# Attention of the first layer rewritten: float32r score operands in two row tiles, a ring of three PSUM banks, no fold on TensorE

## The reference, cut to what matters

```python
q = (xn @ Wq + bq).reshape(B, S, H, dk).transpose(0, 2, 1, 3)
k = (xn @ Wk + bk).reshape(B, S, H, dk).transpose(0, 2, 1, 3)
v = (xn @ Wv + bv).reshape(B, S, H, D).transpose(0, 2, 1, 3)
scores = jnp.einsum('bhsd,bhtd->bhst', q, k) / jnp.sqrt(dk)
p = jax.nn.softmax(scores, axis=-1)
att = jnp.einsum('bhst,bhtd->bhsd', p, v)
out = att.reshape(S, B, D, H).sum(axis=-1).reshape(B, S, D)
```

## Time and profile before

| | us |
|---|---|
| median of 3 runs | 879.9 |
| lowest and highest | 877.4, 882.49 |
| span of the profiled execution | 885.5 |
| TensorE busy | 692.1 |
| VectorE busy | 523.8 |
| ScalarE busy | 306.9 |
| GpSimd busy | 292.2 |

### The profile page before, as it was taken

How to read it: one execution, slowest core, us unless ns; L and a number is a source line. 1 busy time by engine, 2 the same in 40 slices (tenths; PEclk the granted TensorE clock), 3 DMA queues, 4 the chain that set the end, 5 groups by cost and what they waited for, 6 DMA issues and landing times. The chain is left out here.

```text
span 885.5 us, 18398 instructions
## 1 busy us (share of the span) xinstructions
PE 692.1 (78%) x7232; PEld 418.3 (47%) x7232; DVE 523.8 (59%) x898; ACT 306.9 (35%) x563; POOL 292.2 (33%) x369
## 2 busy tenths in 40 slices
PE   4431899999999999969999985986962559746784
PEld 2210334333353444357677764765441548645463
DVE  3572666556666775054545533334899699655873
ACT  2310554446645655522332322553010002122431
POOL 4313041000000023233455451138994000415773
PEclk9665778668898988869999996997896555557987
DMA  3246111111111110000000001001220100000000
GB/s 101 71 139 179 50 45 48 42 36 36 49 53 42 44 47 19 1 0 1 1 1 1 1 1 25 1 14 39 48 49 27 27 4 4 2 0 1 12 13 24
DMA packets 41204, 28.72 MB, mean 32 GB/s; under 512 B 23344, under 2 KB 32560, under 8 KB 41136
## 3 DMA queue, kind: packets, MB, share of 16 engines
q1 hardware_dynamic: 39984, 26.57, 10.6%
q10 hardware_dynamic: 1152, 1.18, 0.4%
HBM read 21.35 MB, written 6.29 MB: 31 GB/s over the span
## 5 line engine op out<-in xcount | busy, mean ns | idle before, releaser
L456 DVE TENSOR_REDUCE mx<-ps 128x1 f32<-128x1024 f32 x128 | 155.7, 1224 | 83.0 <-PE ps L566 80.6
L423 ACT ACTIVATE prob<-ps 128x512 f32<-128x512 f32 x256 | 139.4, 599 | 148.1 <-PE ps L578 146.8
L578 PE MATMUL ps<-qst,kst 99*128 99x512 bf16 x256 | 96.0, 455 | 19.4 <-DMA qst<-shift_sb 19.2
L598 PE MATMUL ps<-prob,vst 128*32 128x256 f32 x1024 | 98.7, 463 | 0.4 <-ACT prob L423 0.4
L717 POOL TENSOR_TENSOR h_lo<-hf,h_hi 128x512 fp32r<-128x512 f32 x48 | 63.6, 1338 | 69.4 <-DVE h_hi L747 69.4
L565 PE MATMUL ps<-km,qm 48*128 48x512 bf16 x128 | 59.1, 463 | 16.4 <-DMA km<-k_scratch 10.0
L578 PEld LDWEIGHTS ps<-qst,kst 99*128 99x128 bf16 x256 | 24.3, 113 | 88.4 <-ACT prob L423 63.1
L608 PEld LDWEIGHTS ps<-fold_sel,q_rest 128*128 128x128 f32 x256 | 62.1, 334 | 7.4 <-issue 7.4
L608 PE MATMUL ps<-fold_sel,q_rest 128*128 128x32 f32 x256 | 64.0, 407 | 0.8 <-ACT q_rest L429 0.8
L791 PE MATMUL ps<-h_hi,w_lo 128*128 128x512 f32 x144 | 58.4, 405 | 7.7 <-issue 5.4
L747 DVE CAST h_hi<-hf 128x512 fp32r<-128x512 f32 x48 | 41.7, 896 | 38.0 <-ACT hf L690 37.4
(11 more groups left out here) (257 smaller groups left out, 1292.0 us busy)
## 6 DMA issues: line engine op xcount, KB each, us to landing
qm<-q_scratch SPq DMA_DIRECT2D x32, 64.0 KB
km<-k_scratch SPq DMA_DIRECT2D x32, 64.0 KB
w_raw<-L_ffn_h_w SPq DMA_DIRECT2D x2, 1024.0 KB, 9.4
q_scratch<-qsplit SPq DMA_DIRECT2D x4, 384.0 KB, 2.5
k_scratch<-ksplit SPq DMA_DIRECT2D x4, 384.0 KB, 2.5
qst<-q_scratch SPq DMA_DIRECT2D x16, 96.0 KB
kst<-k_scratch SPq DMA_DIRECT2D x16, 96.0 KB
X<-L_attn_x SPq DMA_DIRECT2D x4, 256.0 KB, 4.9
```

What stands on the lines that cost most here:

```text
L423: nc.scalar.activation(prob[:, u, :], expp[:, u % 2, :], ACT.Exp, scale=SCORE_SCALE).then_inc(exp_done, 1)
L456: nc.vector.tensor_reduce(mx[:, p, k:k + 1], maxp[:, k % 2, :], AX.X, ALU.max).then_inc(max_done, 1)
L578: nc.tensor.matmul(expp[:, u % 2, :], kst[0:99, p, P * t:P * t + P], qst[0:99, p, 512 * s:512 * s + 512], start=True, stop=True).then_inc( ...
L598: last = nc.tensor.matmul(pvp[32 * j:32 * j + 32, g // 2, cols], vst[:, p, u % 8, :], prob[:, u, cols], start=(g % 2 == 0 and part == 0), ...
```

## The change

The two blocks become one, and everything is written out in 144 steps.

- q and k are kept in two float32r parts (hi from ScalarE, the rest by one VectorE operation out of PSUM). Scratch holds hi, lo, hi of q and hi, hi, lo of k, so that 48 rows give hi*hi + lo*hi + hi*lo. Both matmul kinds use the same operand, which lies twice in SBUF, in rows 0 to 47 and 64 to 111, with two rows of the shift behind each (rows 48, 49 and 112, 113). Four heads' operands fit, one set of 4 DMAs each.
- The two score matmuls of a step (key tile t; queries 0 to 511 and 512 to 1023) use row tiles 0 and 64. Results go in turn to a ring of three banks, which the transposed shift uses as well.
- A value product's four column tiles are four quarters of the queries, accumulated over the eight key tiles, so no fold is needed: VectorE transposes 32 x 32 blocks from PSUM and takes the reciprocal; GpSimd multiplies and adds.
- The maximum comes negated; GpSimd splits the shift in two parts; four DMAs bring it. Scores of head h begin 13 steps behind its first row scores.
- SP issues the FFN's weights ahead of the first shift, and those of the third layer behind it. Score operands of a head are loaded three heads ahead.

```diff
-    q_scratch = nc.dram_tensor("q_scratch", (3, B, P, S), BF16, kind="Internal").ap()
+    q_scratch = nc.dram_tensor("q_scratch", (3, B, P, S), F32, kind="Internal").ap()
...
+    STACKS = 4
+    PROBS = 6
+    RING = 3
+    LAG = 5
+    PV_LAG = 2
+    MAXB, RINGB, PVB = 0, 4, 7
...
+        def score_step(h, t):
+            return 8 * (h + 1) + LAG + t
+
+        def pv_step(h, t):
+            return score_step(h, max(t, 1)) + PV_LAG
+
+        def shift_step(h):
+            return 8 * (h + 1) + 1
...
+            def load_stacks(h):
+                b, p = h // 8, h % STACKS
+                rows = slice(DK0 * (h % 8), DK0 * (h % 8) + DK0)
+                if h % 8 == 0:
+                    sp.wait_ge(splits_stored[2 * b], 4 * 16)
+                    sp.wait_ge(splits_stored[2 * b + 1], 4 * 16)
+                if h >= STACKS:
+                    sp.wait_ge(ring_psum, ring["score", h - STACKS, 7, 1] + 1)
+                for r in (0, 64):
+                    sp.dma_start(qst[r:r + 48, p, :].bitcast(F32), q_scratch[:, b, rows, :]).then_inc(stack_in[p], 16)
+                    sp.dma_start(kst[r:r + 48, p, :].bitcast(F32), k_scratch[:, b, rows, :]).then_inc(stack_in[p], 16)
+
+            def load_shift(h):
+                sp.wait_ge(ring_done, ring["shift", h] + 1)
+                for r in (48, 112):
+                    for j in range(2):
+                        sp.dma_start(qst[r + j:r + j + 1, h % STACKS, :].bitcast(F32),
+                                     shift_sb[8 * j:8 * j + 8, h % 2, :].bitcast(F32)).then_inc(shift_in, 16)
...
+            store_splits(0)
+            store_splits(1)
+            load_stacks(0)
+            store_splits(2)
+            load_stacks(1)
+            store_splits(3)
+            load_stacks(2)
...
+            for o, name in ((W1, "w1"), (W2, "w2")):
+                sp.dma_start(w_raw[:, o:o + FH], dr[f"L0_ffn_{name}_w"]).then_inc(w_in, 16)
...
+            for h in range(NH):
+                load_shift(h)
+                if h + 3 < NH:
+                    load_stacks(h + 3)
...
+            for i, unit in enumerate(ring_order):
+                act.wait_ge(ring_psum, i + 1)
+                if unit[0] == "shift":
+                    h = unit[1]
+                    if h >= 2:
+                        act.wait_ge(shift_in, 64 * (h - 1))
+                    nc.scalar.copy(shift_sb[:, h % 2, :], ps[0:16, RINGB + i % RING, 0:P]).then_inc(ring_done, 1)
+                else:
+                    _, h, t, half = unit
+                    n = 8 * h + t
+                    if n >= PROBS and half == 0:
+                        act.wait_ge(pv_done, n - PROBS + 1)
+                    nc.scalar.activation(prob[:, n % PROBS, GT * half:GT * half + GT], ps[:, RINGB + i % RING, :], ACT.Exp,
+                                         scale=SCORE_SCALE).then_inc(ring_done, 1)
...
+            def split_shift(h):
+                pool.wait_ge(max_done, 8 * (h + 1))
+                if h >= 2:
+                    pool.wait_ge(ring_psum, ring["shift", h - 2] + 1)
+                link(nc.gpsimd.tensor_copy(nsplit[:, h % 2, 0:8], nmx[:, h % 2, :]))
+                nc.gpsimd.tensor_tensor(nsplit[:, h % 2, 8:16], nmx[:, h % 2, :], nsplit[:, h % 2, 0:8].bitcast(F32),
+                                        ALU.subtract).then_inc(shift_split, 1)
+
+            def finish_head(h):
+                pool.wait_ge(folded_ready, 2 * h + 2)
+                f = folded[:, h % 2]
+                link(nc.gpsimd.tensor_tensor(att[:], f[:, :, 0:DK0], rsum[:].rearrange("p (m o) -> p m o", o=1).broadcast_to([P, 8, DK0]), ALU.mult))
+                tile = X[:, h, :]
+                nc.gpsimd.tensor_tensor(tile, tile, att[:].rearrange("p m e -> p (m e)"), ALU.add).then_inc(out_added, 1)
...
+            def left_over(g):
+                dve.wait_ge(q_hi, g + 1)
+                nc.vector.scalar_tensor_tensor(qsp[:, g % 2, 1, :], ps[:, Q_BANK, :], bq[:, 0:1], qsp[:, g % 2, 0, :].bitcast(F32),
+                                               ALU.add, ALU.subtract).then_inc(q_lo, 1)
+                dve.wait_ge(k_hi, g + 1)
+                nc.vector.scalar_tensor_tensor(ksp[:, g % 2, 1, :], ps[:, K_BANK, :], bk[:, 0:1], ksp[:, g % 2, 0, :].bitcast(F32),
+                                               ALU.add, ALU.subtract).then_inc(k_lo, 1)
...
+            def row_max(h, k):
+                s = 8 * h + k
+                dve.wait_ge(max_psum, s + 1)
+                if k == 0 and h >= 2:
+                    dve.wait_ge(shift_split, h - 1)
+                pair = ps[:, MAXB + 2 * (s % 2):MAXB + 2 * (s % 2) + 2, :].rearrange("p c t -> p (c t)")
+                nc.vector.tensor_reduce(nmx[:, h % 2, k:k + 1], pair, AX.X, ALU.max, negate=True).then_inc(max_done, 1)
+
+            def fold(h):
+                dve.wait_ge(pv_done, 8 * (h + 1))
+                if h >= 2:
+                    dve.wait_ge(out_added, h - 1)
+                f = folded[:, h % 2]
+                nc.vector.transpose(f.rearrange("p m e -> p (m e)"), ps[:, PVB, 0:256]).then_inc(folded_ready, 1)
+                dve.wait_ge(folded_ready, 2 * h + 1)
+                if h >= 1:
+                    dve.wait_ge(out_added, h)
+                nc.vector.reciprocal(rsum[:], f[:, :, DK0]).then_inc(folded_ready, 1)
+
+            for step in range(LAST + 2):
+                if step < 8 * NH:
+                    row_max(step // 8, step % 8)
+                for h in range(NH):
+                    if pv_step(h, 7) == step:
+                        fold(h)
...
+            def row_scores(h, k):
+                s, p = 8 * h + k, h % STACKS
                 if k == 0:
+                    pe.wait_ge(stack_in[p], 64 * (h // STACKS + 1))
+                if s >= 2:
+                    pe.wait_ge(max_done, s - 1)
+                bank = MAXB + 2 * (s % 2)
+                nc.tensor.matmul(ps[:, bank, :], qst[0:48, p, P * k:P * k + P], kst[0:48, p, 0:GT], start=True, stop=True)
+                nc.tensor.matmul(ps[:, bank + 1, :], qst[64:112, p, P * k:P * k + P], kst[64:112, p, GT:S],
                                  start=True, stop=True).then_inc(max_psum, 1)
...
+            def shift_to_rows(h):
+                i = ring["shift", h]
+                pe.wait_ge(shift_split, h + 1)
+                if i >= RING:
+                    pe.wait_ge(ring_done, i - RING + 1)
+                nc.tensor.transpose(ps[0:16, RINGB + i % RING, 0:P], nsplit[:, h % 2, :].bitcast(F32), ident[:]).then_inc(ring_psum, 1)
+
+            def scores(h, t):
+                p = h % STACKS
+                if h == 0 and t == 0:
+                    pe.wait_ge(ones_in, 2 * 16)
+                if t == 0:
+                    pe.wait_ge(shift_in, 64 * (h + 1))
+                for half in range(2):
+                    i, r = ring["score", h, t, half], 64 * half
+                    if i >= RING:
+                        pe.wait_ge(ring_done, i - RING + 1)
+                    nc.tensor.matmul(ps[:, RINGB + i % RING, :], kst[r:r + 50, p, P * t:P * t + P], qst[r:r + 50, p, GT * half:GT * half + GT],
+                                     start=True, stop=True).then_inc(ring_psum, 1)
...
+            def pv(h, t):
+                n = 8 * h + t
+                pe.wait_ge(ring_done, ring["score", h, t, 1] + 1)
+                if n == 0:
+                    pe.wait_ge(ones_set, 2)
+                    pe.wait_ge(v_ready, GROUPS)
+                if t == 0 and h >= 1:
+                    pe.wait_ge(folded_ready, 2 * h - 1)
                 for j in range(4):
+                    last = nc.tensor.matmul(ps[32 * j:32 * j + 32, PVB, 0:256], vp[:, h, t, :], prob[:, n % PROBS, 256 * j:256 * j + 256],
+                                            start=(t == 0), stop=(t == 7), skip_group_check=True)
+                last.then_inc(pv_done, 1)
+
+            for step in range(LAST + 1):
+                for h in range(NH):
+                    for t in range(8):
+                        if score_step(h, t) == step:
+                            scores(h, t)
+                if step == shift_step(0):
+
+                    pe.wait_ge(q_lo, GROUPS)
+                    pe.wait_ge(k_lo, GROUPS)
+                    pe.wait_ge(xnT_ready, GROUPS)
+                if step < 8 * NH:
+                    row_scores(step // 8, step % 8)
+                for h in range(NH):
+                    if shift_step(h) == step:
+                        shift_to_rows(h)
+                    for t in range(8):
+                        if pv_step(h, t) == step:
+                            pv(h, t)
```

More of the change, by code:

```diff
@@ L161, in _ @@
+        ring_order = sorted(ring, key=ring.get)
         @block.sync
@@ L244, in _ @@
             rstd(0)
-            for g in range(GROUPS):
-                if g + 1 < GROUPS:
-                    rstd(g + 1)
-                for i in range(2):
-                    pool.wait_ge(q_rounded, 3 * g + i + 1)
-                    src = qf[:] if i == 0 else q_rest[:, 0]
```

(23 more changed lines are left out.)

499 lines of the change are left out of this document (140 added, 359 removed).

## The result

The changed kernel takes 829.4 us (median of 4 runs, 817.6 to 839.1); the kernel before, timed beside it, 880.4 (877.4 to 882.5). The ratio is 0.933, 95% interval 0.925 to 0.941: faster by 51 us in the medians, where 135 were forecast, and 29 us above the top of the range. The profiled execution took 825.4 us at a span of 823.7.

The account below looks back on a forecast made before the run. TensorE was taken to bound the scores' stage. First score 57.5 + steps 170 + last steps 15 + end 3 = 245.5 instead of 380.2, so 885.5 - 134.7 = 750.8 of span, 745 us timed; 8-in-10 range 712 to 800.

Parts of the forecast that it names:

- the stacks of heads 0 to 2: Start, after the stores: SyncE issues these operand loads, 4 issues of 0.7 us each, ending near 39.5 us.
- the change of scale at the end of the sum: End of the sum: profiled span is 5.6 us above the timed median, so 750.8 becomes 745 us.
- The start: Before the scores: first score at 57.5 us instead of 90.8, gaining 33 us; bounds 52 and 66.
- The shift's row: Once a head: arrives 6.1 to 7.1 us after the maximum; TensorE waits 0.8 to 1.8, taken as 0.8.
- The clock: Scores' loop: TensorE at the low level a tenth of the time, adding 0.5 us a head.
- a step: Scores' loop, one step: 1.21 us at 2.4 GHz instead of 1.43; 2.09 at 1.2 GHz instead of 2.52.
- pairs in float32r side by side: Scores' loop: a step's two score matmuls share the array, taking away 0.21 us; weight loads cost nothing extra.
- a head: Scores' loop: 8 x 1.21 + 0.8 + 0.8 = 11.3 us at 2.4 GHz, 11.8 with the low level.
- A: Scores' loop: float32r pairs don't run side by side, 0.43 us more a step, +38: 783 us; chance 0.16.
- B: Scores' loop: less dense streaming lowers TensorE's clock; half the time low 769 us, all 827; chance 0.15.
- C: Scores' loop: VectorE alone sets the pace, 9.85 us a head, -28: 717 us; chance 0.12.
- D: Scores' loop: neither pair shares the array and the clock stays low, 2.95 us a step: 939 us; chance 0.02.

Follow-up runs that it names:

- e5: The change with scratch arrays laid out feature by feature, so a stack load is one run of 48 rows: 752.0 us, ratio 0.855.
- e12: The change, slow stack loads kept, with the shift's four row loads issued by ScalarE instead of SyncE: 868.4 us, ratio 0.985.
- e9: e5 with one small load issued and waited for by SyncE before each head's shift row: 839.5 us, ratio 0.946.
- e13: e9 with 40 extra bf16 matmuls of 128x128 ahead of each head's wait for the shift's row: 791.2 us, ratio 0.900.
- e14: The change, slow stack loads kept, with 40 extra bf16 matmuls ahead of each head's wait for the shift's row: 805.4 us, ratio 0.915.
- e3: The change with 32 bf16 matmuls of 128x128 put ahead of the first score: 817.8 us, ratio 0.924.
- e15: e5 with FFN weight loads behind the shifts of heads 0 to 3, LAG 8, and 32 matmuls ahead of the first score: 733.3 us, ratio 0.833.
- e4: The change with both score matmuls of a step in the first row tile, one behind the other: 919.1 us, ratio 1.046.
- e11: e5 with both score matmuls of a step in the first row tile: 895.5 us, ratio 1.016.
- e7: e5 with two extra bf16 matmuls of 128x128 ahead of each step's row scores: 869.1 us, executions from 809.0 to 910.5.
- e8: e5 with score matmuls contracting 64 rows of each half instead of 50, the extra rows zeros: 752.2 us, ratio 0.856.

## Why the prediction was wrong

**The step that failed** is that of the stacks: "SP then has ... the stacks of heads 0 to 2 (4 issues of 0.7 each ...)". They were priced by their issue and their transport at nothing, in the start and in the loop, and that is 77 of the 84 us by which the time was missed (829.4 to 752.0 by e5 alone; 745 was forecast). The other 7 are the change of scale at the end of the sum: 5.6 us were taken off the span, since the span before was longer than the median of other executions, while e5's profiled execution took 752.5 us at a span of 750.7, 1.7 more. On the scale of the span the forecast was 750.8, and that e5 meets it to 0.1 is luck: its first score comes 2.7 us late, its scores' stage takes 181.0 us in place of 188, and what follows 4.3 more. The profile before had the means to see it: two of its six stack loads a head had a source with the same outermost 3, at half the bytes each, and no row of the forecast is about them. The cost comes in three ways:

- *The start*, 23 us (first exponential 83.7 against 61.0 in e5; the first score was forecast for 57.5 and e5 has it at 60.16). The maxima start 8 us later (43.08 against 34.94), and SP's issues behind the stacks back up: the weights' last issue ends at 77.25 against 52.98.
- *The shift's row*, forecast as 6.1 to 7.1 us from the maximum and a wait of 0.8. In e5 it takes 6.0 (GpSimd's split starts at 113.27, the score at 119.25) and the wait is 0.2 to 0.7; in the change 8.3 (118.91 to 127.22), while a stack trickles in, and the waits were 19.2 us in eleven heads, 1.75 each. Whether the row stands behind the stack's packets in one queue or beside them on the same engines was not told apart, as e12 moved the issues as well.
- *The clock*, forecast low for a tenth of the time. It was low for 46% of the loop (0.77, so 0.23/0.5). This follows from the idle waits: with them gone it was 0.96 (e5), with them put back by a delay alone 0.65 (e9), with them kept and filled 0.98 (e13). The loop of the change was 51 us longer than e5's; at least 20 of these are the clock, since e14 took 20 off with work added, and how the other 31 divide was not measured.

**Right, by e5 or the change:** a step of 1.24 (1.21) and 2.16 at the low level (2.09); pairs in float32r side by side, weight loads of twice the length hidden; no fold; a head of 10.98 us at the high level (11.3, as both stops of TensorE were shorter); two of GpSimd's passes of 0.19 and 0.20 for the split. The stage ends at 241.2 in e5 (245.5). What follows took 509.0 us in place of 505.3, 4 us that the forecast had as unchanged and no run explains. The dropped warming matmuls were overlooked; e3 and e15 differ from the kernels without them by 1% or less, which their runs cannot tell from nothing.

**The rivals.** A (pairs serial, 783) was false, and its price too: made serial, the kernel takes 895.5, as the clock then never leaves the low level. B (clock) named the right quantity, and its sign was there (0.77 in the loop, under 0.8), but with the wrong reason, density. That its price for a clock low all the time, 827, lies beside the measured 829.4 is chance: the clock was low for 46% of the loop, and the late start and the waits made up the rest. The picture beside it from the Trainium skill, "TensorE: Matmul & The Clock Gate", section A second HAM failure mode, short stops between groups in a ring of banks, was not it either: e5 keeps the ring and its short stops at 0.96. C fell: VectorE is at 64% in the change's loop and 81% in e5's. D, two serial pairs at the low level (939), was not run; one serial pair is enough to be slower than before (e4 919.1, e11 895.5, the latter by only 1.6%). It was argued against by "a TensorE that streams all the time at the low level did get the high one back"; e4 and e11 show that it need not.

## What to carry to other kernels

Price every transfer of a loop by its own row: bytes over the GB/s of the stretch in which it runs alone. A share of the DMA engines that stays near a few sixteenths for microseconds, here 3/16, can be a shape to mend and not a load to bear; here the layout of two scratch tensors was worth more than the rewrite of the attention without it (77 us against 51). Whether the kernel before, some of whose loads have an outermost 3 or 2, would gain by it was not tried. And a stop of TensorE can cost more than its length: in e9 24 us more of idle time, 2 to 3 us once a head, came with a loop 93 us longer, because what followed ran at 1.2 GHz. Hide the stop (distance between producer and user), or, where it must stay, fill it; but fill the stop (e13, e14) and not the step (e7).

## What the runs showed of the hardware

- The same 768 KB in four loads: some 10 us, mostly at 66 to 90 GB/s, with an outermost dimension of 3, 4.1 us at 189 GB/s with 48. Four row moves of 4 KB took 6.2 us from the first issue to use while the first kind was under way, 4.3 in e5, where the load before them had ended.
- An issue of one of the shift's rows holds the engine that makes it for 0.65 to 0.68 us, ScalarE as well as SyncE (four in 2.60 and 2.71). An issue of a stack's load took 0.67 to 0.73 us in the change (at 123.92) and 0.32 to 0.42 in e5 (at 118.35), with the same bytes; single issues of SyncE grew to 5.13 us while stores, stacks and weights were all under way.
- A stop of TensorE of 3.19 us (e9, to 113.25) was followed by a score pair of 0.80 us in place of 0.50, and one of 2.43 (e9, to 166.28) by one pair of 0.50 and then ten microseconds at the low level. One of 2.54 (the change, to 127.22) was followed by 22 us at the high level, so a stop of that length does not always bring it down. The stops of 0.2 to 0.7 us once in 11 us in e5 left the loop at 0.96, and waits filled with 2.41 us of matmuls (e13, at 119.31) at 0.98.
- TensorE busy for 321.5 of 323.4 us stayed at 1.2 GHz for all of it (e4, e11), and the profiled execution of e7 was busy for 336.3 of 339.1 us at 0.51, while e5, with the pairs of scores side by side and idle for 9.5 us in 180, ran at 0.96. The Trainium skill, "TensorE: Matmul & The Clock Gate", section Part 1: The HAM clock gate (the "warmup" mystery), has activity release the throttle; by that e11 should have been fast. These rows disagree, and what sets e5 apart from e11 in this is open: padding the rows with zeros made no difference (e8), and the other differences were not tried by themselves.
